# Softmax attention on one core: preparation in half blocks over all positions, and second-pass pieces issued at the position that takes them

## What is computed

```python
probs = softmax(logits)
entropy = sum(-probs * log(probs + 1e-9))
poly = P0*e2*e2 + P1*e2*entropy + P2*e2 + P3*entropy + P4     # e2 = entropy * entropy
beta = where(entropy > 0.5, maximum(poly, 1.0), 1.0)
att = softmax(logits * beta) @ v
x = x + att @ Wo + bo
```

## Time and profile before

| | us |
|---|---|
| median of 3 runs | 2244.32 (2239.89 to 2245.84) |
| the profiled execution | 2240.57 |
| its span, first to last instruction | 2238.8 |
| first pass alone | 754 to 897 |
| both passes | 897 to 1827 |
| second pass alone and last norms | 1827 to 1960 |
| busy in the span | PE 1608.0, DVE 1480.9, ACT 1392.7 |
| granted TensorE clock, mean | 0.762 of 2.4 GHz |

### The profile page before, as it was taken

One profiled execution on the slowest core, in us unless ns is written; L12 is line 12 of the kernel. 1 busy time (PEld: TensorE's weight loads), 2 busy tenths in 40 slices (PEclk: granted clock), 3 DMA queues, 4 the chain that ended last, 5 costly groups with the idle time before them and its releaser, 6 DMA issues. The chain is left out here.

```text
span 2238.8 us, 22322 instructions
## 1 busy us (share of the span) xinstructions
PE 1608.0 (72%) x6402; PEld 689.4 (31%) x6402; DVE 1480.9 (66%) x3478; ACT 1392.7 (62%) x2635; POOL 140.8 (6%) x126
## 2 busy tenths in 40 slices
PE   4787899999999643777776777767787787511166
PEld 2443344444444201222222222223222232201144
DVE  6645354535464798887787887877878773479922
ACT  4564443434333697899987999879999996300012
POOL 0000000000000100000000000000000000035364
PEclk9898899999999755676666766667666778755578
DMA  4000065454556201101011010110110102240031
GB/s 146 0 0 0 14 161 157 130 154 132 155 150 170 59 32 40 62 33 62 24 40 60 33 53 32 35 66 32 43 40 27 48 19 91 58 122 0 0 105 46
DMA packets 56667, 147.36 MB, mean 66 GB/s; under 512 B 7760, under 2 KB 22480, under 8 KB 53936
## 3 DMA queue, kind: packets, MB, share of 16 engines
q1 hardware_dynamic: 52320, 136.63, 20.1%
q0 software_dynamic: 3072, 8.39, 1.2%
q10 hardware_dynamic: 1152, 0.92, 0.3%
HBM read 126.38 MB, written 19.53 MB: 65 GB/s over the span
## 5 line engine op out<-in xcount | busy, mean ns | idle before, releaser
L1682 DVE CUSTOM_DVE_ANT_0 sa_lg<-sa_e,sa_lg 128x1024 f32<-128x1024 f32 (+7 forms) x512 | 386.7, 755 | 89.0 <-ACT sa_lg L1573 88.5
L1673 DVE CUSTOM_DVE_ANT_0 sa_e<-sa_ps,sa_mask 128x1024 f32<-128x1024 f32 (+7 forms) x512 | 385.8, 754 | 76.1 <-PE sa_ps L1423 74.5
L1563 ACT ACTIVATE sa_e<-sa_e,sa_nmax 128x1024 f32<-128x1024 f32 (+7 forms) x512 | 415.2, 811 | 29.2 <-DVE sa_nmax L1673 29.0
L1423 PE MATMUL sa_ps<-sa_space 72*128 72x512 bf16 (+3 forms) x768 | 292.4, 449 | 188.5 <-DVE sa_nmax L1673 142.9
L1573 ACT ACTIVATE sa_lg<-sa_e,sa_sum 128x1024 f32<-128x1024 f32 (+7 forms) x512 | 414.8, 810 | 4.0 <-DVE sa_prod L1682 3.6
L1581 ACT ACTIVATE sa_p<-sa_ps 128x512 f32<-128x512 f32 x576 | 346.9, 629 | 67.2 <-PE sa_ps L1475 37.7
L1472 PE MATMUL sa_ps<-sa_q2s,sa_k2s 75*128 75x512 bf16 (+3 forms) x768 | 295.0, 425 | 69.3 <-ACT sa_p L1581 57.4
L974 DVE TENSOR_TENSOR mx_hw<-mx_spread,mx_h 128x512 f32<-128x512 f32 x256 | 176.1, 691 | 232.2 <-PE mx_ps L813 192.6
L875 ACT ACTIVATE mx_h<-mx_ps 128x512 f32<-128x512 f32 (+1 forms) x264 | 157.0, 597 | 276.7 <-PE mx_ps L800 256.1
L800 PE MATMUL mx_ps<-mx_f,m 128*128 128x512 f32 x512 | 262.0, 597 | 0.8 <-ACT mx_h L875 0.8
L813 PE MATMUL mx_ps<-mx_hw,m 128*128 128x512 f32 x512 | 259.8, 594 | 0.4 <-DVE mx_hw L974 0.4
(11 more groups left out here) (322 smaller groups left out, 1864.6 us busy)
## 6 DMA issues: line engine op xcount, KB each, us to landing
mx_spread<-mx_spill SPq DMA_DIRECT2D x256, 256.0 KB, 4.0
sa_space<-sa_spill_q SPq DMA_DIRECT2D x96, 96.0 KB
sa_space<-sa_spill_k SPq DMA_DIRECT2D x96, 96.0 KB
sa_k2s<-sa_spill_k SPq DMA_DIRECT2D x48, 192.0 KB
sa_q2s<-sa_spill_q SPq DMA_DIRECT2D x48, 192.0 KB
m<-m_in SPq DMA_DIRECT2D x1, 4256.0 KB, 18.4
records<-sa_e SPq DMA_DIRECT2D x8, 512.0 KB, 5.2
be_w<-w_in SPq DMA_DIRECT2D x16, 256.0 KB, 12.1
```

The source lines that it names most:

```text
L1423: last = nc.tensor.matmul(out[:, col:col + w], q_ring[:, c % 2, local, i * P:(i + 1) * P], k_ring[:, c % 2, local, col:col + w], start=Tru ...
L1563: nc.scalar.activation(e[:, u % 5, 0:w], e[:, u % 5, 0:w], ACT.Exp, scale=-1.0, bias=nmax[:, b % 2, i, h:h + 1], accum_out=sums[:, b % 2, ...
L1673: nc.vector.tensor_tensor_reduce(out=e[:, u % 5, 0:w], in0=slot_of("unit", u)[:, 0:w], in1=mask_wide[:, SEQ - w:SEQ], scale=1.0, scalar=3. ...
L1682: nc.vector.tensor_tensor_reduce(out=lg[:, u % 2, 0:w], in0=e[:, u % 5, 0:w], in1=lg[:, u % 2, 0:w], scale=1.0, scalar=0.0, op0=ALU.mult, ...
```

## The change

1. The widening, the steps a, q, k and v of the preparation, `turn_attended` with its copy, and `out_project` with `finish` work on halves (512 columns or four tiles of tokens), each half at a position of its own and with a use of the slot of its own. Semaphores count halves.
2. The preparation's steps are at new positions, in two tables: one for the block after the first, one for the two later ones. The steps of the splits of q and k have one position each.
3. PE issues at position u the pieces that ACT takes at u, no longer those of u + 1; the answers behind them move with them.
4. The widening is at 5 and 7; the steps of the split of the scaled q at 8, 9, 10 (two) and 11. `take_shift` stands behind the pieces of its position on ACT. `turn_attended` is at 13 and 15, the projection at 17 and 19, the bias stays at 11. The last block's scores start two positions later, and so the loop is two positions longer.
5. SP spills q and k at the positions "q_out" and "k_out".

```diff
-LAST_SCORES = FIRST2 + ALL1 + 18
+LAST_SCORES = FIRST2 + ALL1 + 20
-def batch_at(u, r):
-    k, at = divmod(u, UNITS1)
-    return k + 1 if at == r and k + 1 < BATCH else None
+PREPARED = (
+    {"sum": 80, "sub": 81, "square": 83, "var": 84, "root": 86, "scale": 87, "a": (91, 93), "q": (97, 99),
+     "split_q": (101, 102, 104, 105, 107), "q_out": 108, "k": (109, 111), "split_k": (112, 113, 114), "k_out": 112,
+     "v": (115, 117)},
+    {"sum": 12, "sub": 13, "square": 15, "var": 17, "root": 19, "scale": 21, "a": (25, 27), "q": (33, 37),
+     "split_q": (39, 42, 45, 48, 50), "q_out": 51, "k": (53, 57), "split_k": (59, 62, 65), "k_out": 66,
+     "v": (109, 113)})
+def step_at(u, what):
+    b = u // UNITS1 + 1
+    return b if b < BATCH and u % UNITS1 == PREPARED[b > 1][what] else None
...
-        WIDE_AT, SHIFT_AT = 7, 9
-        A_AT, Q_AT, K_AT, V_AT = 83, 87, 89, 107
-        TURN_AT, ATT_AT, PROJ_AT = 9, 13, 17
+        WIDE_AT, SHIFT_AT = (5, 7), 9
+        TURN_AT, BIAS_AT, ATT_AT, PROJ_AT = 9, 11, (13, 15), (17, 19)
+        half_cols = (slice(0, BANK), slice(BANK, SEQ))
+        half_tiles = (slice(0, TILES // 2), slice(TILES // 2, TILES))
...
-                def project(what, weights, b, done):
-                    pe.wait_ge(a_ready.sem, b + 1)
-                    out = take_slot(what, b)
-                    for n in range(HALVES):
-                        cols = slice(n * BANK, (n + 1) * BANK)
-                        last = nc.tensor.matmul(out[:, cols], mat(m3, MATS3, weights), a_cm[:, cols],
-                                                start=True, stop=True)
-                    last.then_inc(done.sem, 1)
+                def project(what, weights, i, done):
+                    b, n = batch_half(i)
+                    pe.wait_ge(a_ready.sem, i + 1)
+                    out = take_slot(what, i)
+                    nc.tensor.matmul(out[:, half_cols[n]], mat(m3, MATS3, weights), a_cm[:, half_cols[n]],
+                                     start=True, stop=True).then_inc(done.sem, 1)
...
-                    for m in pieces2_at(u + 1):
+                    for m in pieces2_at(u):
                         second(m)
                         if m % GROUP == GROUP - 1 and m >= GROUP:
                             answer(m // GROUP - 1)
...
-                    if (k := side_at(u, SHIFT_AT)) is not None:
-                        take_shift(k)
...
                     for m in pieces2_at(u):
                         exp2(m)
+                    if (k := side_at(u, SHIFT_AT)) is not None:
+                        take_shift(k)
...
-                def take_q(b):
-                    dve.wait_ge(q_mm.sem, b + 1)
-                    nc.vector.tensor_scalar(q_cm[b % 2][:, :], slot_of("q", b), -HEAD ** -0.5, None, ALU.mult
-                                            ).then_inc(q_ready.sem, 1)
+                def take_q(i):
+                    b, n = batch_half(i)
+                    dve.wait_ge(q_mm.sem, i + 1)
+                    nc.vector.tensor_scalar(q_cm[b % 2][:, half_cols[n]], slot_of("q", i)[:, half_cols[n]], -HEAD ** -0.5,
+                                            None, ALU.mult).then_inc(q_ready.sem, 1)
```

More of the change, by code:

```diff
@@ L1141, in side_at, with part_at, half_at, batch_half @@
     return k - 1 if at == r and 1 <= k <= SIDES else None
-def batch_at(u, r):
-    k, at = divmod(u, UNITS1)
-    return k + 1 if at == r and k + 1 < BATCH else None
+PREPARED = (
[8 more added lines that the diff above has]
+    return b if b < BATCH and u % UNITS1 == PREPARED[b > 1][what] else None
+def part_at(u, what):
+    b = u // UNITS1 + 1
+    found = PREPARED[b > 1][what] if b < BATCH else ()
+    return (b, found.index(u % UNITS1)) if u % UNITS1 in found else (None, None)
+def half_at(u, what):
+    b, n = part_at(u, what)
+    return None if b is None else 2 * b + n - 1
+def batch_half(i):
+    return divmod(i + 1, 2)
+def twice(found, u, positions):
+    for n, r in enumerate(positions):
+        if (k := found(u, r)) is not None:
+            return 2 * k + n
+    return None
 def group_at(u, r):
@@ L1425, in score, with widen @@
                     last.then_inc(s_mm.sem, 1)
-                def widen(k):
+                def widen(i):
+                    k, n = divmod(i, 2)
                     pe.wait_ge(beta_ready.sem, k + 1)
-                    out = take_slot("wide", k)
-                    for t in range(TILES):
+                    out = take_slot("wide", i)
+                    for t in range(TILES)[half_tiles[n]]:
                         last = nc.tensor.matmul(out[rows_of(k), t * P:(t + 1) * P],
@@ L1511, in turn_attended, with out_project @@
                     last.then_inc(att_t.sem, 1)
[L1513 to L1516, removed]
+                def out_project(i):
+                    b, n = divmod(i, 2)
+                    pe.wait_ge(att_copied.sem, i + 1)
+                    out = tiles_of(take_slot("proj", i))
+                    for t in range(TILES)[half_tiles[n]]:
                         last = nc.tensor.matmul(out[:, t, :], att_cm[:, t * P:(t + 1) * P],
@@ L1817, in _ @@
                         split_shift(k)
-                    if (k := side_at(u, WIDE_AT)) is not None:
-                        widened(k)
-                    for r in (8, 9, 10):
+                    if (i := twice(side_at, u, WIDE_AT)) is not None:
+                        widened(i)
+                    for r, steps in ((8, (0,)), (9, (1,)), (10, (2, 3)), (11, (4,))):
                         if (k := side_at(u, r)) is not None:
-                            split_q2(k, range(2 * (r - 8), min(5, 2 * (r - 8) + 2)))
@@ L1828, in _ @@
                         ln.variance(nc, dve, b - 1, 1)
[L1829 removed]
+                    if (b := step_at(u, "scale")) is not None:
                         ln.scale(nc, dve, b - 1, 1, y_tm[:, :, :])
[L1831 to L1837 removed]
@@ L1838, in _ @@
[L1838 to L1845 removed]
+                    if (i := half_at(u, "a")) is not None:
+                        take_a(i)
```

181 lines of the change are left out of this document (94 added, 87 removed).

## The result

The changed kernel takes 2303.39 us (median of four runs, 2295.70 to 2306.50), against 2245.08 us (2239.89 to 2247.15) for the kernel before on the same chip: a ratio of 1.0258 (1.0237 to 1.0280), 58 us slower. In the profiled executions the span goes from 2238.8 to 2304.7 us, +65.9.

| stretch, us | before | after | difference | predicted |
|---|---|---|---|---|
| all before the attention block | 754.4 | 759.1 | +4.7 | 0 |
| positions 0 to 64 | 90.5 | 90.6 | 0 | 0 |
| 64 to 90 | 62.8 | 54.6 | -8.2 | -3 |
| 90 to 511, both passes | 919.4 | 974.5 | +55.1 | -31 |
| tail, to the last second-pass Exp | 96.1 | 106.7 | +10.6 | +1.5 |

What follows compares the result with a forecast made beforehand. ACT was taken as the bound wherever nothing disturbs it. Terms -3 - 12 - 3 - 12 - 4 + 1.5 = -32.5 us took the profiled 2240.57 us to 2208.1, as median 2212; range 2182 to 2240 us.

Steps and rivals of the forecast that it cites:

- Rival 2: Pieces take the place of the removed waits: at 1.2 us mean stall per extra, 80 us, giving 2261 us; chance 0.10.
- Order of the pieces: Both passes: issuing pieces at their own position costs 0.45 us for each of 67 extras, 30 us for 42.1: -12 us.
- Each stall gives the lead back, so stalls do not follow one another: Both passes: ground for taking 0.45 us per extra, between bounds of 0 and 2.5 us.
- An extra can begin at -0.6 us: PE in both passes: with full lead an extra can begin 0.6 us ahead of ACT's start of its position.
- the lead of 2.5 us: Calm stretches: DVE's row minimum is ready 2.5 us before ACT takes it; ACT stopping in formerly calm stretches would refute this.
- The bank release: PE's 51.1 us in 67 waits on ACT's bank release would go, freeing DVE of waits on scores: lead, not path.
- Halving: DVE work between PSUM and SBUF: 27 x 0.15 = 4 us added, handshakes 23 us, nothing on the path in spare time.
- Spreading: Preparation of blocks: centring -3 us, minimum and product waits -12 us over three preparations, block 1 -3 us.
- Shift: ACT takes the shift behind its position's pieces: its waits fall from 8.9 to 5 us, -4 us.
- Rival 4: PE still stands on slots or banks; 23 us of handshakes eat spreading's gain, time 2238 to 2250 us; chance 0.10.
- Rival 3: DVE stays the bound at positions 12 to 65; 12 of 24 us claimed do not come, 2224 us; chance 0.16.
- Rival 1: Nearly everything hides: pieces cost under 0.2 us per extra, 10 us instead of 30; -58 us, 2186 us; chance 0.22.

Runs made afterwards that it cites:

- e4: The kernel before with only the preparation's steps at the new positions, in whole widths, pieces one position ahead: ratio 0.9844.
- e1: The changed kernel with pieces issued one position ahead again, halves and new positions kept: ratio 0.9938 to the kernel before.
- e3: The changed kernel with pieces at their own position but issued in front of the extras, answers behind: ratio 1.0191 to the kernel before.
- e9: The changed kernel with the answers' products a quarter as wide for all key blocks but the first: ratio 1.0157 to the kernel before.
- e10: The kernel before with the answers' products a quarter as wide for all key blocks but the first, as control: ratio 1.0000.
- e6: e1 with only the preparation halved; widening, attended and projection whole, shift as before: ratio 0.9888 to the kernel before.
- e2: The kernel before with one line changed, pieces issued at their own position; nothing halved or moved: ratio 1.0115.
- e5: e4 with the widening in halves, its split of q in four steps and the shift behind the pieces: ratio 0.9837 to the kernel before.
- e12: e5 with the next position's pieces issued in front of the extras and the answers behind: 2181.88 us, ratio 0.9810 to the kernel before.

## Why the prediction was wrong

**The verdict.** Rival 2 came true, to which I gave 0.10, and larger than its 2261. The parts, by the ratios: spreading in whole widths -35 us (e4), halves +21 (e1 against e4), order of the pieces +72 (after against e1), in sum +58.

**Order of the pieces, the step that failed.** I forecast 30 us of waits for 67 extras, 0.45 each; measured are 123.7 us, 1.85 for each extra, far beyond the 0.95 at which I said the change is worth nothing. Two steps of it broke.

"Each stall gives the lead back, so stalls do not follow one another" is the larger: 43.8 us of waits come one position behind an extra and 16.2 later still, 60 us for which the forecast had nothing. A stall of ACT does give DVE its lead (median 3.2 us one position behind an extra, for 1.3 before), but PE has its own backlog: the answer of 1.90 us and the next scores stand before the next piece. e3 shows how a delay passes on to the next position, and e9 that the answers are part of it (22 us of time, probably more); the control e10 shows that the old order pays nothing for them.

"An extra can begin at -0.6 us" is the other: it took the lead of 2.5 us from unit 170 in a calm stretch. 54 extras start at 0.01 us on average and stop ACT 0.57 us each at their own position, near my 0.45. The 12 halves of the widening start at +1.98 on average and stop ACT 2.75 us each, 33.0 us, and I had priced them like the rest. In front of the first half DVE's temperature work has used up the lead; the second comes late behind an answer.

So much for the waits. That the order costs 72 us in the changed kernel and 26 in the kernel before is measured; how the 72 split over the two steps is not, since waits pass from one position to the next and no run takes one step alone.

**Calm stretches.** I named a stopped ACT there as a refutation of the lead of 2.5 us. It does not stop: the stretch 1188 to 1220 shows 31.63 of 32 us busy, but the missing 0.37 are the first part of a wait of 0.50 us at the turn of position 223, with which the stretch ends; up to 1219 ACT is busy 31.00 of 31.00 us. More than eight positions behind an extra the lead is 2.4 us in the kernel before and 2.6 in the changed one (medians). The lead was right where I read it, and it was gone where DVE had extra work.

**The bank release.** I called PE's 51.1 us of stand lead, not path, and rightly, but drew the wrong conclusion. A PE that stands because ACT's bank is full is a PE that is ahead. With the new order that stand turned into waits of PE for DVE's minimum (69.4 to 136.4 us), and DVE's wait for scores, which I expected "well under 72 us", is 90.1.

**Halving.** The added DVE time is as small as priced (5.9 us in all). "Nothing on the path" was wrong: 0.94% with pieces ahead, about 21 us, of which some 10 for the preparation (e6). In the profiles of e4 and e1 it is 11.0 us more of waits for pieces in both passes, and 3.7 us of tail: more than DVE's time for the added work.

**Spreading.** Right in kind and near in size: in e4 the waits for minimum, product and centred rows fell from 26.7 to 14.4 us, -12.3 for my -3 and -12. What I had not counted is that the pieces gain as well, 41.0 to 25.6 us. Block 1 gave -8.2 us, not -3. By the ratio it is -35 us in all. In after itself the minimum's waits went to nothing, but e2 shows that the order alone does that, so the zero is no proof of the spreading.

**Shift.** Right in direction: I had 8.9 to 5 us, and it is 3.0 in e1 and 3.8 in e5. The zero in after is no proof, since e2 has it too, with the shift in its old place.

**SP and the spills.** Nothing, as predicted: ACT waits for no load in the stretch.

**Tail.** +1.5 predicted, +10.6 and +3.1 measured. ACT's waits there, 1879 to 2010:

```profile
ACT sa_p L1620 <- PE sa_ps L1512: 20.5, 8, 9.3
ACT sa_p L1620 <- PE sa_ps L1509: 15.9, 9, 4.4
```

They sum to 36.4 us, for 24.8 before. The column "tail" shows the cause: 94.8 with neither, 98.5 with halves, 98.6 with the order, 106.7 with both. I priced the halves alone and left the order out of the tail.

**The rivals.** Rival 4's added handshakes cost time (halves), but PE's stands on banks did go. Rival 3 does not show: the minimum no longer stops ACT. Rival 1 asked for full lead, which isn't there at the widening, and for stalls that end with their position. For rival 2 I had the right deciding number and argued against it with a row of full-width extras; the missing step was to follow one extra through PE's whole queue, two positions on.

## What to carry to other kernels

Here an engine that stood because its consumer's buffer was full held a lead; issuing its work just in time removed that wait and put the producer's delays on the path. Before you move work later in an in-order queue, take the worst extra, not a calm stretch. Ask when its last input comes, what stands behind it up to the item that the consumer takes after the next, and whether that fits in what the consumer leaves. Look at every kind of extra: one trace of one kind would have missed the widening. Try the parts of a change one by one: here spreading gained 1.6%, and one index in the order lost 3.2%.

## What the runs showed of the hardware

Four fp32 products of 128x9 weights, each onto 32 output partitions of its own, run beside each other: where three of the four are left out, the one that stays takes as long as the four (234.4 us for 576 products, 231.3 for 1536). The Trainium skill (TensorE: Matmul & The Clock Gate, Part 3: Packing small matmuls) has three column tiles, of 32 outputs each, at 2.38 times the speed. The busy times here agree in direction; no run here has such products one after another, so none measures the speedup.

Less work on PE came with a lower granted clock: with about half of the answers' time (200.9 to 106.5 us, 204.6 to 104.8) it went from 0.67 to 0.54 in e9 and e10, towards the level of 1.2 GHz (0.5 of full speed). In e9 PE's busy time fell by 12 us where the answers' fell by 94. In e12, whose ACT idles least, it is 0.69.
